# The cross-attention mask: written to the scores' bank by ScalarE instead of added by a third matmul

## The reference

```
Q, K, V = heads of (xn @ W_q.T), (ctx @ W_k.T), (ctx @ W_v.T)     16 heads of 16 features, 77 context rows
scores  = Q K^T / 4,  where(mask, scores, -1e10)                   256 x 77 per head
out     = softmax(scores) V @ W_proj.T + bias
```

## Time and profile before

| what | value |
|---|---|
| median of 3 runs | 1597.21 us (1596.92 to 1598.76) |
| the profiled execution's own time | 1600.0 us |
| its span, first to last instruction | 1598.2 us |
| PE matmul busy | 1517.5 us (95%) |
| DVE busy | 1221.1 us (76%) |
| ACT busy | 986.8 us (62%), 2671 instructions |
| POOL busy | 825.6 us (52%) |
| mean granted TensorE clock | 0.986 of full speed |

### The profile page before, as it was taken

How to read it: one execution, slowest core, us unless ns; L and a number is a source line. 1 busy time by engine, 2 the same in 40 slices (tenths; PEclk the granted TensorE clock), 3 DMA queues, 4 the chain that set the end, 5 groups by cost and what they waited for, 6 DMA issues and landing times.

```text
span 1598.2 us, 32435 instructions
## 1 busy us (share of the span) xinstructions
PE 1517.5 (95%) x10912; PEld 1356.7 (85%) x10912; DVE 1221.1 (76%) x3060; ACT 986.8 (62%) x2671; POOL 825.6 (52%) x937
## 2 busy tenths in 40 slices
PE   3599999999999999999999999999999999999986
PEld 3478888998888989888898989889888988988864
DVE  3767788878778887877888787788887778888643
ACT  2466666666666666666666666666666666666641
POOL 3354655555465555556554555655465565546320
PEclk9989999999999999999999999999999999999987
DMA  5000000000000000000000000000000000000000
GB/s 144 1 12 13 19 19 18 18 10 13 19 19 19 18 17 7 17 19 19 19 18 16 7 18 19 19 19 18 16 6 19 19 19 19 18 16 6 10 9 14
DMA packets 88819, 29.56 MB, mean 18 GB/s; under 512 B 68304, under 2 KB 88656, under 8 KB 88656
## 3 DMA queue, kind: packets, MB, share of 16 engines
q1 hardware_dynamic: 88656, 27.49, 7.4%
HBM read 16.55 MB, written 8.39 MB: 16 GB/s over the span
## 4 chain that ended last, share of the span: by engine, by line
PE 68%; DVE 11%; issue 9%; POOL 8%; ACT 3%; SPq 0%; DMA 0%; POOLq 0%; ACTq 0%; DVEq 0%
PE bank L389 56%; DVE a_conv L818 8%; PE bank L395 6%; PE bank L623 3%; POOL a_Er_lo L1392 2%; POOL a_qkr L1399 2%; POOL a_o L1430 2%; DVE x_nmax L943 1%; ACT a_Er_hi L1165 1%; PE bank L702 1%; PE bank L477 1%; ACT x_prob L1264 0%; DVE a_rC L840 0%; SPq L379 0%; ACT x_Q_stack L1251 0%
## 5 line engine op out<-in xcount | busy, mean ns | idle before, releaser
L1264 ACT ACTIVATE x_prob<-bank,x_nmax 128x77 f32<-128x77 f32 x1024 | 249.0, 331 | 144.0 <-DVE x_nmax L943 143.8
L943 DVE TENSOR_REDUCE x_nmax<-bank 128x4 f32<-128x308 f32 x256 | 121.2, 474 | 132.0 <-PE bank L389 129.2
L389 PE MATMUL bank<-x_Vbd,x_probT 128*128 128x34 f32 (+1 forms) x1280 | 164.9, 265 | 0.2 <-ACT x_probT L1275 0.2
L389 PEld LDWEIGHTS bank<-x_Vbd,x_probT 128*128 128x128 f32 x1280 | 163.0, 193 | 0.3 <-ACT x_probT L1275 0.3
L818 DVE SCALAR_TENSOR_TENSOR a_conv<-a_raw,cw,a_conv 128x256 f32<-128x256 f32 x384 | 154.9, 478 | 9.3 <-POOL a_conv L1387 9.3
L1275 ACT ACTIVATE x_probT<-bank 128x256 f32<-128x256 f32 (+1 forms) x256 | 112.8, 441 | 70.6 <-PE bank L623 70.6
L1392 POOL TENSOR_TENSOR a_Er_lo<-a_E,a_Er_hi 128x512 fp32r<-128x512 f32 x32 | 41.5, 1296 | 178.4 <-ACT a_Er_hi L1165 178.4
L623 PE MATMUL bank<-ident,x_prob 128*128 128x128 f32 x640 | 115.1, 278 | 1.5 <-ACT x_probT L1275 1.5
L840 DVE RECIPROCAL a_rC<-bank 128x512 f32<-128x512 f32 x32 | 107.1, 3346 | 3.4 <-PE bank L389 3.4
L389 PE MATMUL bank<-x_K_bd,x_Q_stack 128*128 128x308 f32 x256 | 92.7, 362 | 7.6 <-ACT x_prob L1264 6.0
L843 DVE TENSOR_TENSOR a_AT<-bank,tri 128x512 f32<-128x512 f32 x128 | 87.1, 681 | 14.0 <-PE bank L389 13.0
(11 more groups left out here) (254 smaller groups left out, 5537.1 us busy)
## 6 DMA issues: line engine op xcount, KB each, us to landing
x<-in_x SPq DMA_DIRECT2D x32, 256.0 KB, 2.7
out<-x SPq DMA_DIRECT2D x32, 256.0 KB, 2.1
ctxT<-in_ctxT SPq DMA_DIRECT2D x32, 77.0 KB, 2.0
x_Vbd<-x_Vtok SPq DMA_DIRECT2D x128, 9.6 KB
keep<-in_mask SPq DMA_DIRECT2D x32, 19.2 KB, 2.0
f_s<-in_fWu SPq DMA_DIRECT2D x2, 256.0 KB, 5.7
x_Vbd<-x_Vtok SPq DMA_DIRECT2D x32, 6.0 KB
x_Vbd<-x_Vtok SPq DMA_DIRECT2D x32, 3.6 KB
```

Of the source, the lines that this page charges most:

```text
L389: return pe.matmul(out, lhsT, rhs, start=start, stop=stop, skip_group_check=True)
L943: dve.tensor_reduce(nmax[:, u % 2, :], X0[:, 0:UH * S2].rearrange("p (h s) -> p h s", h=UH), AX.X, ALU.min).then_inc(on.x_max, 1)
L1264: ins = act.activation(prob[:, col:col + S2], X0[:, i * S2:(i + 1) * S2], ACT.Exp, scale=-1.0, bias=nmax[:, u % 2, i:i + 1])
```

## The change

The third matmul and its operand `ident_bf` are gone. ACT has a new step `x_pre`: it copies `negmask` (bf16 in SBUF, broadcast over four heads) to `X0`, 128x308 float32, ahead of each unit. The two score matmuls are issued with `start=False`, so that they add to what stands in the bank. For this the second half of `x_q` is issued with `start=False` as well. `x_s` now waits for `x_pre` of its own unit and for nothing of `x_prob`; `x_pre` waits for `x_prob` of the unit before (its own engine), or, for unit 0, for `x_ql` and `x_neg`. In ACT's list `x_pre` of unit 0 stands directly behind `x_q` and ahead of `a_xnt`, and each other `x_pre` directly behind the `x_prob` that frees the bank. No other step is moved.

```diff
-            def mm_halves(dst, pairs):
+            def mm_halves(dst, pairs, fresh=True):
                 n = len(pairs)
                 for i, (lhsT, rhs) in enumerate(pairs):
-                    mm(dst, lhsT(0), rhs(0), start=(i == 0), stop=False)
+                    mm(dst, lhsT(0), rhs(0), start=(fresh and i == 0), stop=False)
...
             def x_q(r):
...
-                        for k in range(KC)])
+                        for k in range(KC)], fresh=(j == 0))
...
             def x_s(r, u):
...
                     pe.wait_ge(on.x_kbd, upto(r))
-                    pe.wait_ge(on.x_neg, upto(r))
-                else:
-                    pe.wait_ge(on.x_prob, upto(r, NU, u))
+                pe.wait_ge(on.x_pre, upto(r, NU, u + 1))
                 out = X0[:, 0:UH * S2]
-                mm(out, Q_stack[:, q, c * P:(c + 1) * P], K_bd[:, q], stop=False)
-                mm(out, Q_stack[:, q, c * P:(c + 1) * P], KT_lo_bd[:, f, hh:hh + UH, :], start=False, stop=False)
-                mm(out, ident_bf[:], negmask[:, c:c + 1, :].broadcast_to([P, UH, S2]), start=False
+                mm(out, Q_stack[:, q, c * P:(c + 1) * P], K_bd[:, q], start=False, stop=False)
+                mm(out, Q_stack[:, q, c * P:(c + 1) * P], KT_lo_bd[:, f, hh:hh + UH, :], start=False
                    ).then_inc(on.x_s_ps, 1)
...
+            def x_pre(r, u):
+                if u == 0:
+                    act.wait_ge(on.x_ql, upto(r))
+                    act.wait_ge(on.x_neg, upto(r))
+                else:
+                    act.wait_ge(on.x_prob, upto(r, NU, u))
+                c = u // QU
+                act.activation(X0[:, 0:UH * S2].rearrange("p (h s) -> p h s", h=UH),
+                               negmask[:, c:c + 1, :].broadcast_to([P, UH, S2]), ACT.Copy).then_inc(on.x_pre, 1)
...
-                F(f_xnt); X(x_q); N(a_xnt); X(x_prob, 0); N(a_raw_qk); F(f_lgt); A(a_oke); X(x_prob, 1)
-                F(f_th, 0); N(a_raw_v); X(x_pt, 0); F(f_gap); X(x_prob, 2); A(a_qnt); N(a_e); X(x_prob, 3)
-                X(x_pt, 1); N(a_gt); X(x_pt, 2); X(x_prob, 4); N(a_convt, 0); N(a_ehi); A(a_osq); F(f_st, 0)
-                X(x_prob, 5); X(x_pt, 3); F(f_th, 1); N(a_convt, 1); X(x_prob, 6); X(x_pt, 4); X(x_prob, 7)
-                X(x_pt, 5); X(x_pt, 6); A(a_ot); X(x_pt, 7); F(f_st, 1); N(a_qbd)
+                F(f_xnt); X(x_q); X(x_pre, 0); N(a_xnt); X(x_prob, 0); X(x_pre, 1); N(a_raw_qk); F(f_lgt)
+                A(a_oke); X(x_prob, 1); X(x_pre, 2); F(f_th, 0); N(a_raw_v); X(x_pt, 0); F(f_gap)
+                X(x_prob, 2); X(x_pre, 3); A(a_qnt); N(a_e); X(x_prob, 3); X(x_pre, 4); X(x_pt, 1); N(a_gt)
+                X(x_pt, 2); X(x_prob, 4); X(x_pre, 5); N(a_convt, 0); N(a_ehi); A(a_osq); F(f_st, 0)
+                X(x_prob, 5); X(x_pre, 6); X(x_pt, 3); F(f_th, 1); N(a_convt, 1); X(x_prob, 6); X(x_pre, 7)
+                X(x_pt, 4); X(x_prob, 7); X(x_pt, 5); X(x_pt, 6); A(a_ot); X(x_pt, 7); F(f_st, 1); N(a_qbd)
```

More of the change, by code:

```diff
@@ L60 @@
     "a_qnT a_P_ps a_P a_o_ps a_osq a_oss a_ove a_orinv a_o1 a_o2 a_oT_ps a_oT a_wo_ps a_x1 "
-    "x_k_ps x_v_ps x_q_ps x_k x_kl x_kbd x_v x_q x_ql a_xnTl x_xnTl f_xnTl a_Ehi a_Elo a_oTl x_oTl f_sTl x_neg x_s_ps x_max x_prob x_pT_ps x_pT "
+    "x_k_ps x_v_ps x_q_ps x_k x_kl x_kbd x_v x_q x_ql a_xnTl x_xnTl f_xnTl a_Ehi a_Elo a_oTl x_oTl f_sTl x_neg x_pre x_s_ps x_max x_prob x_pT_ps x_pT "
     "x_av_ps x_rs x_o x_oT_ps x_oT x_x1b x_proj_ps x_x2 f_gate_ps f_lgT f_lg_ps f_logit f_top f_topi f_topf "
@@ L86, in build @@
         ident = sb("ident", [P, P])
-        ident_bf = sb("ident_bf", [P, P], BF16)
         tri_r = sb("tri", [P, P], F32R)
@@ L746, in _ @@
             pe.wait_ge(ld_w, W_LANDED)
-            pe.wait_ge(w_ready, 4)
+            pe.wait_ge(w_ready, 3)
             pe.wait_ge(w_hi, len(splits))
@@ L1096, in _ @@
             dve.tensor_copy(tri_r[:], tri_raw).then_inc(w_ready, 1)
-            dve.tensor_copy(ident_bf[:], ident[:]).then_inc(w_ready, 1)
             split(splits, 0)
             dve.wait_ge(z_ready, 4)
-            dve.wait_ge(w_ready, 4)
+            dve.wait_ge(w_ready, 3)
             iterations(body, others)
@@ L1340, in others @@
                 act.wait_ge(ld_v, V_LANDED)
-                act.wait_ge(w_ready, 5)
+                act.wait_ge(w_ready, 4)
                 split(other_splits)
@@ L1498, in _ @@
             pool.wait_ge(ld_w, W_LANDED)
-            pool.wait_ge(w_ready, 4)
+            pool.wait_ge(w_ready, 3)
             iterations(body, others)
```

## The result

The changed kernel takes 1657.86 us (median of 4, 1654.48 to 1664.88) against 1597.07 us (1595.01 to 1598.76) in the same comparison: a ratio of 1.0387, interval 1.0349 to 1.0425. That is 60.8 us more. The forecast was 43 more with an upper end of 1657: the sign and the places of the loss were right, the size was too small and the range missed by 0.9 us. With more executions, in another comparison, it was 1660.16 us (1655.70 to 1667.76), ratio 1.0390 (1.0365 to 1.0415). Intervals are 95% intervals of the ratio.

A forecast was written before the change was run, and what follows sets the result against it. PE's queue was taken to bound one part of a body, a chain over DVE, ACT and POOL the other. +1.27 us a body over 29 bodies (36.8) plus 6 made 43 us more: 1640 us, 8-in-10 range 1612 to 1657.

The forecast's parts named there:

- What bounds the kernel: PE's queue sets the time from `a_ot` to `a_P`; from `a_P` to `a_ot` the chain runs over DVE, ACT, POOL.
- the walk: Step-by-step count of lateness through one body, unit 0 to unit 7, summing to +1.27 us a body.
- The price of the copy: Each 128x308 mask copy on ACT into PSUM was taken at 0.43 us, bounds 0.275 and 0.50.
- "dear write": Rival: ACT's write into PSUM takes 0.6 us instead of 0.43; +1.95 us a body, 1660 us; chance 10%.
- Unit 0 ... 0.97 us late: `a_xnt` on ACT held behind `x_ql` and the copy makes DVE and PE's `a_qk` 0.97 us late.
- Units 1 to 3 save 3 x 0.145 = 0.43. Nothing else waits: Three removed mask matmuls on PE each save 0.145 us, 0.43 in all, with no new wait.
- unit 4's delay: PE loses 0.35 us because unit 4's scores wait for `x_prob` 3 and the copy.
- unit 5's push: `x_pre` 5 on ACT pushes `a_convt` 0 and steps up to `x_prob` 5; 0.21 us in the sum.
- unit 6's delay: Unit 6's scores wait for late `x_prob` 5 and the copy, starting 1.42 us late; 0.46 in the sum.
- The clock: Rival: PE's pauses bring the lower clock for 5 us of each body's work; 80 us more, 1720 us; chance 3%.
- the forecast's own signs of being wrong: A body under 47.3 us, `a_qk` less than 0.7 us late, or granted clock below 1.00 in steady bodies.
- Filling and draining, "6": Three further bodies with an `X` stage, where fewer other steps hide a unit, cost 6 us together.

The follow-up runs named there:

- the late units: Mask written by ACT only for units 4, 6, 7, others by matmul as before: 1609.62 us, ratio 1.0075; only for unit 5: 1608.69 us, 1.0070.
- the wait alone: Kernel before with no mask write; only ACT waits for `x_ql` ahead of `a_xnt`: 1615.07 us, ratio 1.0113.

## Why the prediction was right in kind and too small

- **What bounds the kernel, and that a push on ACT costs in full from `a_P` to `a_ot`:** right. From unit 4 to `a_ot` the trace has 0.80 us more (1.59 - 0.79), where the walk had 0.73, and ACT's part of the chain rose from 3% to 12%. Run by themselves the late units gave 0.30 and 0.22.
- **The price of the copy:** right, 0.432 us; ScalarE writing to PSUM was no dearer than the rows of reading from it had said. The estimate from the Trainium skill's figures ("ScalarE: Activation LUTs", What ACT_TABLE_LOAD costs), 0.443, lies 0.011 above the measured time. The "dear write" rival falls. That four of them stand in the sum: right (4.0).
- **"Unit 0 ... 0.97 us late":** mis-sized, 1.09 in the trace and 1.08 in its own run (the figures of the walk give 839.80 - 838.84 = 0.96). I let `a_xnt` start 0.10 us before the end of the copy, as ACT's steps usually do. It started 0.03 behind that end (871.30, 871.33). The run with the wait alone has a surplus too: +0.60 where the arithmetic for a copy of no length gives 0.53. Why this step does not overlap, while those behind the writes of units 1 to 6 start 0.06 to 0.07 early, no run here shows.
- **"Units 1 to 3 save 3 x 0.145 = 0.43. Nothing else waits":** this step failed. From `a_qk` (1.09 late) to the masked `a_P` on DVE (884.66 - 32.03 = 852.63 against 851.84, 0.79 late) only 0.30 came back, the matmuls of units 1 and 3. The timelines of PE and DVE show where the third stayed: `a_qt`, `a_s` and the second `a_P` on DVE, in the kernel before and then in the kernel after.

```profile
845.77 0.60 PE L395 MATMUL bank<-ident,a_qn 128*128 128x128 f32 x4
846.25 0.38 PE L389 MATMUL bank<-ws_hi,a_xnT_hi 128*128 128x256 f32 x1
...
851.84 0.69 DVE L843 TENSOR_TENSOR a_AT<-bank,tri 128x512 f32<-128x512 f32 x1 [0.17 <-PE bank L389]
```

```profile
878.59 0.60 PE L394 MATMUL bank<-ident,a_qn 128*128 128x128 f32 x4
879.22 0.39 PE L388 MATMUL bank<-ws_hi,a_xnT_hi 128*128 128x256 f32 x1
...
884.66 0.69 DVE L839 TENSOR_TENSOR a_AT<-bank,tri 128x512 f32<-128x512 f32 x1 [0.17 <-PE bank L388]
```

Behind unit 2 `a_qt` is 0.79 late (878.59 - 32.03 against 845.77), but `a_s` is 0.94 late: the 0.15 us is lost there. `a_s` waits for `a_raw_v` on ACT, and starts 0.06 us behind its end before (845.59 + 0.60) and 0.05 behind it after (878.57 + 0.60), so it had nothing to gain. The matmul of unit 2 lay beside the hand-over from `a_v` over ACT to `a_s`, and its own runs give it 0.05. I had looked only at the wait for the scores themselves, not at what PE does between `a_v` and `a_s`.
- With the terms as the trace has them, a body's sum is 1.09 - 0.30 + 0.33 (unit 4's delay) - 0.09 (its matmul) + 0.24 (unit 5's push) + 0.43 (unit 6's delay) - 0.12 (its matmul) = 1.58, the measured 1.57 within rounding. Of the 0.3 us beyond the forecast's 1.27, the two errors above make 0.25. The parts run alone add up to less, 1.08 - 0.25 + 0.30 + 0.22 = 1.35: alone, a late `x_prob` 4 still falls into ACT's wait for the convolution (0.22 us idle ahead of `a_convt` in the run of units 1 to 3), and with unit 5's write behind it that cover is gone. That is argued from the traces; units 4 and 5 together were not run.
- **The clock**, which the sum put at nothing, with a rival at 3% and a price of 80 us: this is the second step that failed, and one of the forecast's own signs of being wrong came true. The mechanism of the rival was there, and its price was wrong. It is not a matter of all bodies or none; four of 28 fell, for 3.4 us each, at 1.6 us apiece. (The price was mis-added as well: 5 us of work at twice the time is 5 us more a body and not 2.5; the 2.5 belongs to 5 us that pass at the lower level.) The Trainium skill ("TensorE: Matmul & The Clock Gate", A second HAM failure mode: psum-queue depth-cycling) tells of a kernel in which short idle times between groups of matmuls bring the lower clock back again and again. The trace agrees in this, at two pauses of 0.45 and 0.83 us. My argument against it, a stretch with 1.1 us of 5 idle at full clock, showed only that such a pause need not do it; every long body here stands beside three short ones with the same pause. The other stretch of those rows, 75 to 80 us at 0.50, sets no bound either: the clock had fallen ahead of it (0.81 from 71 to 73 us), in a pause of PE of 4.94 us.
- **Filling and draining, "6":** 9 us. The size was taken from the links of the steady body. Whether the rest is links that less other work hides, or the lower clock there, was not shown.
- The errors in the body (0.3 us, 9 us in all), the clock (6) and the filling (3) make up the 18 us missing.

## What to carry to other kernels

Before an added step is put ahead of others in an engine's strict order, ask what it waits for: here the wait alone, without its 0.43 us of work, cost 0.60 us a body, because the step behind it had been ready long before. When work is moved off the busiest engine, go through each moved piece and ask what ran beside it; of eight removed matmuls only those of units 1 and 3 gave back their time where PE was short of it, unit 2's covered a hand-over, and those of units 4 and 6 gave 0.09 and 0.12 us each behind a longer delay. Where units differ in slack, treat them differently: the same edit for units 1 to 3 alone gives 0.996 to 0.998 of the old time, for all eight 1.039.

## What the runs showed of the hardware that I had not expected

- The granted clock fell in four of 28 bodies, each fourth one from the seventh to the nineteenth, at `a_qk`, in both profiled executions, and for 3.4 us each time, after pauses of under 1 us with PE 92% busy over the span. With unit 0's write alone, where the pause is as long, no steady body fell. What decides between them is open.
- Nine idle matmuls in that pause held the clock in the one execution that was profiled, and took nothing from the body: 48.27 us with and without them.
- The step behind the one write that had waited for another engine did not overlap with it; behind the writes of units 1 to 6, which waited only for ACT's own `x_prob`, the next step began 0.06 to 0.07 us before their end.
